# A softmax-sum addition per chunk moved from VectorE to GpSimd, in two attention layers run as one pipeline

## What is computed

```python
def layer0(x):            # group norm, 8 heads of 32 channels
    h = groupnorm(x, groups=32) * gn_w + gn_b
    q, k, v = split(qkv_w @ h + qkv_b)
    w = softmax((q * scale).T @ (k * scale), axis=keys)   # 8 x 1024 x 1024 per image
    return x + proj_w @ (v @ w.T) + proj_b

def layer1(x):            # one head, 32 channels for q and k, 256 for v
    w = softmax((Wq @ x).T @ (Wk @ x), axis=keys)         # 1024 x 1024 per image
    return gamma * ((Wv @ x) @ w.T) + x
```

## Time and profile before

| | before |
|---|---|
| median of the runs (lowest, highest) | 1796.03 us (1795.3, 1802.6) |
| the profiled execution | 1793.55 us, span 1791.7 us from first to last instruction |
| granted TensorE clock, mean | 0.930 of full speed |
| TensorE busy | 1579.1 us (88%) |
| VectorE busy | 1368.8 us (76%) |
| GpSimd busy | 1153.9 us (64%) |
| ACT busy | 821.2 us (46%) |

### The profile page before, as it was taken

The page is one execution under the profiler, slowest core; times in us unless marked ns, Lnnn a source line. Parts: engine busy times, 40 slices in busy tenths (PEclk is TensorE's granted clock), DMA queues, the critical chain, the costliest instruction groups (busy, mean ns, idle before and its releaser), DMA issues.

```text
span 1791.7 us, 25554 instructions
## 1 busy us (share of the span) xinstructions
PE 1579.1 (88%) x7120; PEld 900.4 (50%) x7120; DVE 1368.8 (76%) x1884; ACT 821.2 (46%) x1501; POOL 1153.9 (64%) x528
## 2 busy tenths in 40 slices
PE   4988888998989979899799989899898997988868
PEld 2534443664445734466345654357444573445337
DVE  2889798868888678877897688886788869785343
ACT  2255445534455345544455435553445534543402
POOL 2278666756867467675676658675676757776804
PEclk8699989998999989999899989999899999998979
DMA  5223030301303023030411104030130303100100
GB/s 127 55 65 71 2 94 19 72 7 42 97 19 72 18 55 89 1 72 18 112 32 37 37 23 121 19 72 13 36 97 19 72 18 79 41 1 7 42 18 24
DMA packets 38745, 85.77 MB, mean 48 GB/s; under 512 B 10304, under 2 KB 20416, under 8 KB 38592
## 3 DMA queue, kind: packets, MB, share of 16 engines
q1 hardware_dynamic: 38208, 82.88, 18.4%
q0 software_dynamic: 384, 1.05, 0.3%
HBM read 18.29 MB, written 8.39 MB: 15 GB/s over the span
## 4 chain that ended last, share of the span: by engine, by line
PE 63%; DVE 19%; issue 12%; SPq 2%; ACT 2%; DMA 1%; DVEq 0%; POOL 0%; ACTq 0%; POOLq 0%
PE pv L494 13%; PE st L463 11%; PE work L517 10%; PE pv L472 10%; DVE mpart L812 9%; PE work L585 5%; DVE rec L904 3%; PE work L549 3%; PE work L561 3%; PE work L592 2%; PE work L555 2%; PE st L455 2%; SPq L325 1%; DVE attn L908 1%; PE work L538 1%
## 5 line engine op out<-in xcount | busy, mean ns | idle before, releaser
L788 POOL TENSOR_TENSOR acc<-acc,probs 128x1024 f32<-128x1024 f32 x352 | 836.9, 2408 | 166.6 <-ACT probs L651 166.4
L651 ACT ACTIVATE probs<-st 128x512 f32<-128x512 f32 x1152 | 618.9, 598 | 577.3 <-PE st L463 439.9
L812 DVE TENSOR_REDUCE mpart<-work 128x1 f32<-128x512 f32 x1024 | 645.2, 679 | 189.0 <-PE work L517 187.5
L517 PE MATMUL work<-ks,qs 96*128 96x512 f32 x1024 | 417.5, 488 | 69.5 <-DVE mpart L812 59.4
L463 PE MATMUL st<-qs,ks 98*128 98x512 f32 x1024 | 378.8, 450 | 26.2 <-ACT probs L651 13.2
L463 PEld LDWEIGHTS st<-qs,ks 98*128 98x128 f32 x1024 | 184.0, 198 | 290.0 <-ACT probs L651 155.6
L788 POOL TENSOR_TENSOR acc<-probs 128x1024 f32<-128x1024 f32 x64 | 152.3, 2390 | 246.9 <-ACT probs L651 246.9
L517 PEld LDWEIGHTS work<-ks,qs 96*128 96x128 f32 x1024 | 204.7, 206 | 184.1 <-DVE mpart L812 105.9
L472 PE MATMUL pv<-probs,vt 128*32 128x512 f32 x2048 | 286.4, 632 | 0.9 <-ACT probs L651 0.9
L494 PE MATMUL pv<-probs,l_vt 128*128 128x256 f32 x1024 | 254.1, 384 | 5.6 <-ACT raw L724 5.2
L494 PEld LDWEIGHTS pv<-probs,l_vt 128*128 128x128 f32 x1024 | 190.6, 191 | 44.5 <-issue 9.9
(11 more groups left out here) (77 smaller groups left out, 1134.2 us busy)
## 6 DMA issues: line engine op xcount, KB each, us to landing
qs<-part_hi SPq DMA_DIRECT2D x124, 128.0 KB, 2.4
ks<-part_hi SPq DMA_DIRECT2D x124, 128.0 KB, 2.4
xa<-in_x SPq DMA_DIRECT2D x16, 512.0 KB, 4.2
qs<-part_lo SPq DMA_DIRECT2D x64, 128.0 KB, 2.4
ks<-part_lo SPq DMA_DIRECT2D x64, 128.0 KB, 2.5
y<-in_x SPq DMA_DIRECT2D x8, 1024.0 KB, 5.3
out<-raw SPq DMA_DIRECT2D x32, 256.0 KB, 2.2
qs<-mrow SPq DMA_DIRECT2D x256, 2.0 KB
```

The source lines that it names most:

```text
L517: last = mm(bank, qs[g][0:HI_HI_LO, j, t0:t0 + P], ks[g][0:HI_HI_LO, j, half * HALF:(half + 1) * HALF], start=True, stop=True)
L651: nc.scalar.activation(probs[:, n % PRING, half * HALF:(half + 1) * HALF], st[:, (2 * n + half) % ST_BANKS, :], ACT.Exp).then_inc(s_exp1 i ...
L788: pool.tensor_tensor(a, first, probs[:, n % PRING, :], ALU.add).then_inc(s_add0, 1)
L812: last = dve.reduce_max(mpart[:, 4 * j + tb, half:half + 1], bank, AX.X)
```

## The change

VectorE's entry "A" is taken out of the plans of all kinds of pass and out of VectorE's program. GpSimd no longer leaves out the last block's second pair, so it makes all 14 additions of a chunk, in the order of the units. The semaphore `s_addv` goes; `s_add0` now counts 14 per chunk and is the only one that SUM and ACT wait for. The table `MAXIMA_OF_SLOT` is only wrapped anew; its 72 numbers are the same.

```diff
 STEADY = {
     "maxima1": (19, 19, 24, 24, 26, 28, 28, 31, 32, 32, 33, 34, 34, 37, 38, 42, 43, 44),
-    "last_block": (0, 16, 33, 50),
...
     if kind == "epilogue":
-        plan[0].append(("A", 3))
...
     chains = {
-        "last_block": [("A", ci) for ci in (3, 0, 1, 2)],
...
-        s_addv = sem("s_addv")
...
-        ADDS0 = 13 * 4
+        ADDS0 = 14 * 4
...
         def wait_added(eng, i, b):
 
             ci, blk, pair = i // 16, i % 16 // 2, i % 2
-            if blk == SB - 1 and pair == 1:
-                eng.wait_ge(s_addv, 4 * b + ci + 1)
-            else:
-                eng.wait_ge(s_add0, ADDS0 * b + 13 * ci + 2 * (max(blk, 1) - 1) + pair + 1)
+            eng.wait_ge(s_add0, ADDS0 * b + 14 * ci + 2 * (max(blk, 1) - 1) + pair + 1)
...
-                    pe.wait_ge(s_add0, 13 * n_acc)
-                    pe.wait_ge(s_addv, n_acc)
+                    pe.wait_ge(s_add0, 14 * n_acc)
...
                 if kind == "epilogue" and n < L1_AT + PRING:
                     act.wait_ge(s_pv0, 32 * B)
-                    act.wait_ge(s_addv, 4 * B)
+                    act.wait_ge(s_add0, ADDS0 * B)
...
                     ci, blk, pair = i // 16, i % 16 // 2, i % 2
-                    if blk == 0 or (blk, pair) == (SB - 1, 1):
+                    if blk == 0:
                         continue
...
-                elif e[0] == "A":
-                    ci, pair = e[1], 1
-                    bb = b - 1 if ci == 3 else b
-                    i = 16 * ci + 14 + pair
-                    dve.wait_ge(s_exp0, 2 * (L0_UNITS * bb + i + 1))
-                    wait_added(dve, i - 2, bb)
-                    n = last_slot(ci) - 1 + pair
-                    a = acc[:, ci % 2, pair, :]
-                    dve.tensor_tensor(a, a, probs[:, n % PRING, :], ALU.add).then_inc(s_addv, 1)
```

More of the change, by code:

```diff
@@ L36 @@
 PIECE = HALF // PIECES
-MAXIMA_OF_SLOT = (0, 3, 3, 2, 3, 1, 4, 1, 3, 1, 1, 3, 1, 2, 4, 2, 0, 1, 4, 0, 0, 1, 5, 1, 2, 3, 2, 5, 0, 3, 4, 0, 0, 1, 1, 0,
-                  3, 1, 3, 2, 2, 2, 1, 4, 0, 2, 5, 1, 2, 1, 0, 3, 0, 4, 3, 1, 2, 2, 2, 0, 2, 0, 3, 6, 0, 0, 3, 1, 1, 1, 4, 2)
+MAXIMA_OF_SLOT = (0, 3, 3, 2, 3, 1, 4, 1, 3, 1, 1, 3, 1, 2, 4, 2, 0, 1, 4, 0, 0, 1, 5, 1, 2, 3, 2, 5, 0, 3, 4, 0, 0,
+                  1, 1, 0, 3, 1, 3, 2, 2, 2, 1, 4, 0, 2, 5, 1, 2, 1, 0, 3, 0, 4, 3, 1, 2, 2, 2, 0, 2, 0, 3, 6, 0, 0,
+                  3, 1, 1, 1, 4, 2)
 STEADY = {
     "maxima1": (19, 19, 24, 24, 26, 28, 28, 31, 32, 32, 33, 34, 34, 37, 38, 42, 43, 44),
-    "last_block": (0, 16, 33, 50),
     "qk1": (59, 63, 67, 67, 67, 69),
@@ L117, in plan_of @@
         for e, n in zip(chains[name], slots):
-            of_before = name in ("sums1", "layer1", "maxima1") or e[:3] in (("SUM", 1, 1), ("R", 1, 1)) or e == ("A", 3)
+            of_before = name in ("sums1", "layer1", "maxima1") or e[:3] in (("SUM", 1, 1), ("R", 1, 1))
             of_after = name in ("norm", "split0", "qk1", "v0") or (name == "maxima" and e in of_next)
@@ L122, in plan_of @@
     return plan
-NO_BANK = ("MC", "MC1", "BN", "AGG", "NORM", "H", "HL", "A", "R", "R1")
+NO_BANK = ("MC", "MC1", "BN", "AGG", "NORM", "H", "HL", "R", "R1")
 SCALAR_USES = ("QK", "VT", "VT1", "SUM", "SUM1")
```

## The result

| | before | after |
|---|---|---|
| median (lowest, highest) | 1796.03 us (1794.21, 1802.6) | 1811.57 us (1809.8, 1814.36) |
| ratio, 95% interval | | 1.0081 [1.006, 1.0101] |
| profiled execution | 1793.55 us, span 1791.7 | 1811.02 us, span 1809.2 |
| VectorE busy | 1368.8 us | 1336.6 us |
| GpSimd busy | 1153.9 us | 1221.3 us |

The changed kernel is slower by 15.5 us, twice the 7.4 us that were forecast and 0.6 us above the stated range. VectorE's busy time fell by 32 us, less than the 63 us of its additions, as was forecast; 16 of the missing 31 us are the multiplication L850, whose eight executions grew from 9.9 to 25.8 us together.

A forecast was written before the change was run, and what follows sets the result against it. TensorE was busy 88% of the span with 63% of the chain, VectorE 19%. Terms +6.6 + 1.3 + 0.5 - 0.8 - 0.2 = +7.4 us on the 1796.03 us median gave 1803.4 us, range 1789 to 1811.

The forecast's parts named there:

- The covers: At each chunk's end, slack hides GpSimd's longer queue from sums, exponentials and its next addition: costed at nothing there.
- The term that was to decide: End of chunk 0, six steady images: GpSimd's longer run holds L850, making TensorE 1.1 us late each, +6.6 us.
- rival 1: At chunk 0's end L850 is let in between two GpSimd additions: 1794.7 us; chance 0.30.
- rival 2: After L850, the normalization's last multiplications are caught by GpSimd's next addition: 13.8 us more, 1817.2 us; chance 0.10.
- rival 3: Freed VectorE reaches L908 before GpSimd's additions, saving 5.5 us in six images: about 1762 us; chance 0.07.
- Image 0: L850 held up to 113.38, sums and exponentials +2.35 us, normalization meeting GpSimd's next addition: +1.3 us for chunk 0.
- The small gains: Chunk 2 of image 0 +0.5 us, start of the last image -0.8, epilogue -0.2.
- The rule that was weighed: VectorE/GpSimd shared pair: the blocked engine enters when the first's instruction finishes; by it the L850 term would be 0.

The follow-up runs named there:

- m123: Changed kernel with only the last additions of chunks 1, 2 and 3 moved to GpSimd, chunk 0's left with VectorE: 1793.56 us, ratio 0.9978 to before.
- after_psum2: Changed kernel with PSUM operands for both the 128x2 multiplication and VectorE's next short operation, so neither has two SBUF inputs: 1795.35 us, ratio 0.9971 to before.
- m0: Changed kernel with only chunk 0's last addition moved to GpSimd, those of chunks 1 to 3 left with VectorE: 1811.37 us, ratio 1.0078 to before.
- gap15: Changed kernel in which GpSimd's last addition of every chunk also waits for the one just before it: 1797.13 us, ratio 1.0 to before.
- m0_first: Kernel before with chunk 0's last addition moved to GpSimd in image 0 only: 1804.09 us, ratio 1.0019 to before.
- after_psum: Changed kernel with only the 128x2 multiplication's second operand placed in PSUM: 1809.54 us, ratio 1.0068 to before.
- extra0_run: Kernel before plus one GpSimd addition ending chunk 0, reading constants and not waiting for GpSimd's preceding addition: 1806.07 us, ratio 1.005 to before.
- m3: Changed kernel with only chunk 3's last addition moved to GpSimd, the others left with VectorE: 1793.49 us, ratio 0.9976 to before.
- extra0: Kernel before plus one GpSimd scratch addition ending chunk 0, which waits for the addition just before it: 1797.29 us, ratio 0.9998 to before.
- gap_all: Changed kernel in which every GpSimd addition but a chunk's first waits for the one just before it: 1713.03 us, ratio 0.9549 to before.

## Why the prediction was right and wrong

- *The covers held.* In the trace of the kernel after no SUM waits for GpSimd. SUM, the exponentials and GpSimd's next addition were costed at nothing, and m123 and after_psum2, with three and four longer queues per image, are not slower than before. ACT's waits for GpSimd's additions, which were to grow by no more than 5 us, fell from 37.6 to 16.4 us.
- *The term that was to decide did, and its mechanism is shown.* L850 ends with GpSimd's run (3.28 us in image 4, forecast 3.30 us), TensorE's second fill follows at once, and each steady image is 1.0 us late at slot 16: 6.2 us, forecast 6.6. m0 (the one addition), gap15 (the gap) and after_psum2 (the operands) show it from three sides. With L850's median at 3262 ns, rival 1 falls for this operation.
- *The further loss of rival 2 did not come.* The normalization's last operation started 0.42 us before GpSimd's next addition (942.50 and 942.92), 0.28 us before the change: both had slipped, as was argued. Nor did rival 3: the product that it wanted to shorten takes 6.26 us in every steady image, against 6.25 before.
- *Image 0 was mis-sized, and its working was wrong in two places.* The forecast had +1.3 us for chunk 0. The multiplication took 6.13 us as worked out, but the exponential of slot 18 then comes 3.9 us later and not 2.35: TensorE stands idle 3.99 us instead of 1.91, and its stretch at 1.2 GHz (granted clock 0.50) comes 3.3 us earlier, so that the product after it takes 1.94 us instead of 1.06. For the same reason GpSimd's next addition starts at 118.67 and not at 117.1, and the normalization, done by 117.55, is not caught by it. At slot 20 nothing is left of the delay (123.70 against 124.07). What the forecast did not have is the next meeting: an attn product that was let in after one addition before the change is held over four, and from slot 26 on the image is some 9 us late. First the kernel before, then after:

```profile
131.37 1.46 DVE L908 TENSOR_TENSOR attn<-attn,rec 128x512 f32<-128x512 f32 x1
```
```profile
130.98 8.63 DVE L901 TENSOR_TENSOR attn<-attn,rec 128x512 f32<-128x512 f32 x1
```

By the image's end it is 10.1 us. Whether that belongs to the change is open. In all five traces in which chunk 0's run of image 0 is longer and without a gap (after, m0, m0_first, after_psum, extra0_run) this product is held for 8.6 us; of the seven others without the wait before every addition, six let it in (1.5 to 1.7 us) and m3, which leaves chunk 0 alone, does not. But m3's profiled execution took 1801.94 us, 8 us more than its median of ten, so the product may fall either way from one execution to the next. The medians of ten give the change in image 0 3.4 us [0.2, 6.8] (m0_first).
- *The small gains* (chunk 2 of image 0, the last image, the epilogue) summed to -0.5 us; m123 has -4 us [-7.6, -0.4] for chunks 1 to 3. Its place was not sought further.
- *The sum.* 6.2 to 7.4 us in the steady images and some 3.4 in image 0, less what chunks 1 to 3 give back, makes 6 to 11 us. The measured 15.5 us (its interval 10.8 to 18.1) is more, and m0 alone has 14. The intervals of the parts are wide enough to cover the difference; if there is one, what the few microseconds are stays open. The forecast's steady term was right, and its miss lies in image 0 and in this rest.
- *The loop's turns.* The projection at 1.2 GHz in five turns of after against two of before is not the change's doing: extra0, where VectorE keeps its additions and which is as fast as before, comes late by 1.6 to 1.7 us at the same three turns, and m3's turns are slow as well. Of all the traces that of before has the fewest slow turns. Their clock, kernel after and kernel before at the turn into image 5 (us, busy times of PE, PEld, DVE, ACT and POOL, granted clock, DMA share, GB/s):

```profile
1109.00:1113.00 4.00, 3.97 (x8) 2.19 (x9) 0.52 (x1) 1.27 (x3) 3.48 (x2) 0.68 0.73 165
```
```profile
1091.00:1095.00 4.00, 3.83 (x15) 2.16 (x19) 2.92 (x3) 2.17 (x4) 0.59 (x1) 1.00 0.81 184
```

- *The rule that was weighed.* The Trainium skill (SBUF — State Buffer, section "Who interferes with whom") says that whoever issues first has the shared pair for the whole instruction; by that the blocked side would be let in when this instruction finishes. In gap_all the trace agrees: no operation of VectorE with two SBUF inputs takes over 2.2 us more than the shortest of its form, which is less than one addition. In a run of additions without a gap it often does not agree (L850 was held over two and three additions), and there the trace is what counted.

## What to carry to other kernels

Moving work off a busy engine onto an idle one can cost by what the receiving engine's longer run does to others, even where its own queue has slack, as here. Where GpSimd and VectorE both work on SBUF, look at the longest against the shortest duration of one VectorE form (here 8601 against 691 ns): a large ratio points to such waiting, and its cure may be a wait, placed where GpSimd's next operation would follow without a gap. If an experiment that frees one instruction changes nothing, look whether the next instruction has taken over its wait before dropping the theory.

## What the runs showed of the hardware that was not expected

- A wait of GpSimd for its own preceding addition costs it little (mean of an accumulating addition 2402 ns in after, 2434 in gap_all) and lets VectorE in: a gap of 0.08 us was enough in extra0. Without it VectorE often stays out to the end of the run, 13.9 us in the worst row of before, over the six additions that were left of a run:

```profile
222.03 13.92 DVE L895 TENSOR_TENSOR part_lo<-part_lo,part_hi 128x1024 fp32r<-128x1024 f32 x1
```

- Whether an operation is let in at the first end of an addition is not fixed by the order of issue: L908 met two like runs 1.2 us after an addition had begun and took 8.60 us once and 1.70 us once. Once it was kept out at one end, it was kept out to the end of the run in all rows of before and after that I compared. Of the operations of before with two SBUF inputs that met a run of additions without a gap, 23 were kept out over at least one more addition and 37 were let in at the end of the addition that they met: the prediction's "mostly waits to the end of the run" holds for L850 and for 19 of 23 such meetings of L908, not for all such operations. Why some pass was not settled.
- Operations of 128x2 are held to the end of a run as those of 128x1024 are (6.13 us for L850 in image 0 of after, where it takes 0.16 us unheld); one operand in PSUM was enough to let them through (0.16 us in a run).
